# A four-layer graph network kernel: a list sorted by source on the chip, fp32 sums by node, one attention pass

## What is computed

```python
# L0: hyperbolic linear map per node, then a plain sum over the edges
xt = logmap0(proj(mobius_add(proj(mobius_matvec(w, h)), bias)))
x += expmap0(relu(logmap0(proj(expmap0(segment_sum(xt[src], dst))))))
# L1: attention with 4 heads, then 25 steps of a spiking neuron
e = leaky_relu(a_src[src] + a_dst[dst], 0.2); p = exp(e - max_of_destination(e))
x += lif(segment_sum(xw[src] * p, dst) / segment_sum(p, dst) + b) + h
# L2: four edge types; both directions; edges with src == dst left out
x += sum over t of  segment_sum(h[src] * m_t, dst) @ WA[t]  and  segment_sum(h[dst] * m_t, src) @ WB[t], plus x terms
# L3: two graph convolutions with edge weights w (and a loop of weight 1), layer norm behind each
deg = segment_sum(w, dst) + 1; out = dinv * (segment_sum(w * (dinv*h)[src], dst) + dinv*h) + b
```

## Time and profile before

| | |
|---|---|
| median of 3 runs | 9762.14 us (9749.57 to 9762.45) |
| the profiled execution: span from first to last instruction | 9752.6 us |
| busy: PE / weight loads / DVE / ACT / POOL | 3033.5 / 2507.1 / 4339.8 / 1537.8 / 5945.4 us |
| DRAM read / written | 554.98 / 177.15 MB |
| mean granted clock of TensorE, as a share of full speed | 0.559 |

### The profile page before, as it was taken

The page is one execution under the profiler, slowest core; times in us unless marked ns, Lnnn a source line. Parts: engine busy times, 40 slices in busy tenths (PEclk is TensorE's granted clock), DMA queues, the critical chain, the costliest instruction groups (busy, mean ns, idle before and its releaser), DMA issues.

```text
span 9752.6 us, 141440 instructions
## 1 busy us (share of the span) xinstructions
PE 3033.5 (31%) x30372; PEld 2507.1 (26%) x30373; DVE 4339.8 (44%) x10248; ACT 1537.8 (16%) x3193; POOL 5945.4 (61%) x5419
## 2 busy tenths in 40 slices
PE   1122224555311443332232222323242222222221
PEld 1111114555301331012222222222242222222221
DVE  5311135666535997975222222222244333443334
ACT  1000012222101555710111111111120000100000
POOL 0677735777302990007888888888826777367773
PEclk7555557777655555565555555555575555555555
DMA  5322214455322330012333333333343222132221
GB/s 140 84 79 79 79 36 112 133 135 134 96 57 62 99 98 4 1 68 58 61 61 61 61 61 61 61 61 61 61 122 83 78 79 78 38 82 78 78 78 52
DMA packets 578212, 733.23 MB, mean 75 GB/s; under 512 B 158774, under 2 KB 437770, under 8 KB 578138
## 3 DMA queue, kind: packets, MB, share of 16 engines
q0 software_dynamic: 306176, 438.23, 21.0%
q1 hardware_dynamic: 242010, 267.02, 9.4%
q10 hardware_dynamic: 29952, 27.28, 1.1%
HBM read 554.98 MB, written 177.15 MB: 75 GB/s over the span
## 4 chain that ended last, share of the span: by engine, by line
issue 28%; DVE 19%; POOL 15%; PE 15%; DVEq 11%; DMA 8%; ACT 2%; SPq 0%; ACTq 0%; POOLq 0%
POOL GATHERED L599 11%; PE PS L755 8%; DVEq L318 6%; POOL agg_src L665 5%; DMA GATHERED<-typed_tab,IDX 4%; DVE OH L1350 3%; DVE H L1549 2%; DMA agg_src<-MSG,SIDX 2%; PE PS L884 2%; DVE SCR L1344 2%; DVE T L1148 1%; PE PS L809 1%; DVE SM L1158 1%; DVEq L321 1%; DMA GATHERED<-gat_tab,IDX 1%
## 5 line engine op out<-in xcount | busy, mean ns | idle before, releaser
L599 POOL DMA_INDIRECT GATHERED<-row_tab,IDX x2496 | 2372.0, 950 | 1430.6 <-issue 1139.5
L755 PE MATMUL PS<-OH,GATHERED 128*128 128x64 bf16 (+1 forms) x15760 | 1161.1, 253 | 2509.6 <-DVE OH L1350 1561.5
L755 PEld LDWEIGHTS PS<-OH,GATHERED 128*128 128x128 bf16 x15760 | 1022.5, 132 | 2605.9 <-DVE OH L1350 1625.5
L665 POOL DMA_INDIRECT agg_src<-MSG,SIDX x832 | 1331.9, 1601 | 266.8 <-issue 211.4
L599 POOL DMA_INDIRECT GATHERED<-typed_tab,IDX x832 | 879.0, 1056 | 992.0 <-ACT IDX L965 738.9
L599 POOL DMA_INDIRECT GATHERED<-gat_tab,IDX x832 | 785.1, 944 | 452.2 <-issue 229.9
L876 PE MATMUL PS<-EQ,OH 128*128 128x128 bf16 x1024 | 145.7, 294 | 1946.6 <-issue 1707.1
L809 PE MATMUL PS<-IDENT,GATHERED 128*128 128x128 f32 x3328 | 598.7, 356 | 465.9 <-DMA GATHERED<-gat_tab,IDX 349.5
L1807 DVE TENSOR_TENSOR ACC<-ACC,PS 128x128 f32 x256 | 73.7, 288 | 1354.4 <-PE PS L755 1354.4
L809 PEld LDWEIGHTS PS<-IDENT,GATHERED 128*128 128x128 f32 x3328 | 540.4, 187 | 523.9 <-issue 523.8
L969 ACT ACTIVATE IDX<-SRCF 128x4 int32 x816 | 166.9, 205 | 2980.8 <-DMA GATHERED<-row_tab,IDX 2980.8
(11 more groups left out here) (279 smaller groups left out, 6615.0 us busy)
## 6 DMA issues: line engine op xcount, KB each, us to landing
gat_rows<-GATHERED SPq DMA_DIRECT2D x208, 264.0 KB, 2.1
GATHERED<-gat_rows SPq DMA_DIRECT2D x208, 264.0 KB, 2.6
GATHERED<-row_tab,IDX POOLq DMA_INDIRECT x2496
ROWI<-dst_rows ACTq DMA_DIRECT2D x208, 128.0 KB, 3.1
ROWI<-dst_rows SPq DMA_DIRECT2D x208, 128.0 KB, 2.9
ROWI<-key_rows SPq DMA_DIRECT2D x208, 128.0 KB, 3.1
agg_src<-MSG SPq DMA_DIRECT2D x2, 12564.0 KB, 77.3
H<-agg_src SPq DMA_DIRECT2D x98, 256.0 KB, 3.9
```

The source lines that it names most:

```text
L599: pool.indirect_dma_start(out=rows, out_offset=None, in_=table, in_offset=bass.IndirectOffsetOnAxis(ap=IDX[:, k:k + 1], axis=0),).then_inc ...
L665: pool.indirect_dma_start(out=agg_src[k], out_offset=bass.IndirectOffsetOnAxis(ap=SIDX[:, u * CT + t:u * CT + t + 1], axis=0), in_=MSG[:, ...
L755: last = mm(bank(0)[:, 0:o.shape[1]], row_part(t, i), o, start=(n == 0 and t == 0), stop=(n == len(groups) - 1 and t == CT - 1))
```

## The change

- **Sums by node, fp32.** One-hots are 128 x 512 fp32 over a whole block of 128 nodes, and are the stationary operand; the gathered fp32 rows (512 bytes) are the moving one. PE's result has a node on a partition and is added to ACC, T or X directly. `split`, the parts, the windows of 64 and `unload` go. In l0 a column with the edge weight rides along for the degree. In l3 ACT multiplies each gathered row by its weight in place (`weighed_rows`).
- **A list sorted by source.** During walk l0 DVE counts the edges per block of sources (first half: a compare and a reduce over 832 columns every second chunk), works out the starts, and ranks them (second half: a compare, a scan and two more operations of 832 columns every second chunk). POOL then scatters (key, source) pairs, 8 bytes a row, to their places with 832 indirect DMAs, in batches of 16: 96 between l0 and g1 (LISTED_EARLY), 352 behind g1's gathers, 384 when the attention pass is over. Before a batch POOL copies indices and pairs aside and waits for the last batch of the same kind (`listed`).
- **The second typed direction is a walk** ("l2b") over that list: a second typed table is made during walk l2, a block per four chunks (`typed_b`), and gathered by destination and type. `same_keys`, the scatter-add, the copies in DRAM and "back" go. Both walks add straight into X.
- **One attention pass.** "ga", the scores and "gb" become one walk: ACT makes the transposed one-hots (Abs, Relu), PE spreads maxima and scores, DVE does the four small score steps of a chunk (`score`), ACT the Exp, DVE the product (`weigh`), PE and DVE the sums. Where a chunk reaches into a second block, its one-hots and sums are made ahead in buffers of their own (`two`).
- **Typed table.** One fp32 copy per block, even blocks by ACT, odd ones by DVE.
- **Registers.** `read` loads four words; each is passed through a maximum with zero (`kept`) wherever it is used.

```diff
+    typed_b_tab = dram("typed_b_tab", (NB * P * NT4, D))
+    list_dram = dram("list_dram", (NT * P, 2))
...
+                for t in range(BATCH):
+                    pool.indirect_dma_start(out=list_dram,
+                                            out_offset=bass.IndirectOffsetOnAxis(
+                                                ap=PLACE_NOW[:, now + t:now + t + 1], axis=0),
+                                            in_=REC_NOW[:, rec + 2 * t:rec + 2 * t + 2],
+                                            in_offset=None).then_inc(listed[k], 16)
...
+            pool.wait_ge(placed, 1)
+            list_batches(0, LISTED_EARLY)
+            pool.wait_ge(s_stored, 32)
+            walk("g1", gat_tab, XW)
+            list_batches(LISTED_EARLY, LISTED_BESIDE)
+            pool.wait_ge(walks["gb"].added, NCH + 2)
+            list_batches(LISTED_BESIDE, NT // (2 * BATCH))
+            for k in range(SLOTS):
+                pool.wait_ge(typed_stored[k], 16 * (NG * len(range(k, GB, SLOTS)) + 1))
+            walk("l2", typed_tab, D)
+            pool.wait_ge(nb_stored, 16 * (NB + 1))
+            walk("l2b", typed_b_tab, D)
...
-                    pool.tensor_tensor(VROWS[u].rearrange("p (t h d) -> p t h d", t=CT, h=HEADS),
-                                       G3[:, u * CT:(u + 1) * CT, 0:D].rearrange("p t (h d) -> p t h d", h=HEADS),
-                                       EX[:, bass.ds(c * (CT * HEADS), CT * HEADS)]
-                                       .rearrange("p (t h o) -> p t h o", h=HEADS, o=1)
-                                       .to_broadcast([P, CT, HEADS, DH]), ALU.mult).then_inc(v_made, 1)
...
-                            pool.indirect_dma_start(out=agg_src[k],
-                                                    out_offset=bass.IndirectOffsetOnAxis(
-                                                        ap=SIDX[:, u * CT + t:u * CT + t + 1], axis=0),
-                                                    in_=MSG[:, m * P:(m + 1) * P], in_offset=None,
-                                                    compute_op=ALU.add).then_inc(scattered[k], 16)
...
+                pe.wait_ge(ready, k + 1)
+                for t in range(CT):
+                    r = rows(t)
+                    last = mm(bank(to + p)[:, 0:r.shape[1]], onehots_(p, t), r, start=(t == 0), stop=(t == CT - 1))
...
+                    mm(bank(3), NB_HT, WL2[:, (NT4 + 1) * D:(2 * NT4 + 1) * D], start=True, stop=True).then_inc(nb_mm, 1)
+            aggregate("l2", gathered("l2"), gathered_row, parts=((NB, typed_b, None), (NIT - NB, None, None)))
+            aggregate("l2b", gathered("l2b"), gathered_row, table=RANGES_SRC)
...
+                        for t in range(CT):
+                            rows = G3[:, u * CT + t, 0:D]
+                            last = nc.scalar.activation(rows, rows, ACT.Copy, scale=WF[:, bass.ds(c * CT + t, 1)])
+                        last.then_inc(row_weighed, 1)
...
+                nc.scalar.activation(SCRB[:, CE:2 * CE], ROWI[:, u * CE:(u + 1) * CE], ACT.Abs,
+                                     bias=NODE[:, bass.ds(first, 1)], scale=float(FAR)).then_inc(far_made, 1)
+                hold(act, far_made, c + 1)
+                hold(act, adm_ready, c + 1)
+                nc.scalar.activation(EQB[:, p * CE:(p + 1) * CE], SCRB[:, CE:2 * CE], ACT.Relu,
+                                     bias=ONE[:, :], scale=-1.0).then_inc(ot_ready, 1)
...
+            def weights_of(c, u):
+                hold(act, scored, 5 * c + 6)
+                nc.scalar.activation(VX[:, u * CT:(u + 1) * CT, D:XW],
+                                     SCORE[:, (u % 2) * CT * HEADS:(u % 2 + 1) * CT * HEADS]
+                                     .rearrange("p (t h) -> p t h", h=HEADS), ACT.Exp).then_inc(ex_kept, 1)
...
+            def same_bucket(k):
+                return v.tensor_scalar(SAME, BUCKET, KCOL[:, bass.ds(k, 1)], None, ALU.is_equal)
...
+                    v.tensor_reduce(TOTALS[:, bass.ds(k, 1)], SAME, axis=AX.X, op=ALU.add).then_inc(counted, 1)
...
+                    same_bucket(k).then_inc(ranked, 1)
+                    hold(dve, ranked, 4 * k + 2)
+                    v.tensor_tensor_scan(BEFORE, ONE[:, :].to_broadcast([P, NT]), SAME, OFFSETS[:, bass.ds(k, 1)],
+                                         ALU.mult, ALU.add).then_inc(ranked, 1)
+                    hold(dve, ranked, 4 * k + 3)
+                    v.tensor_tensor(BEFORE, BEFORE, SAME, ALU.mult).then_inc(ranked, 1)
+                    hold(dve, ranked, 4 * k + 4)
+                    v.tensor_tensor(PLACEF, PLACEF, BEFORE, ALU.add).then_inc(ranked, 1)
...
+                at_edges(AT3, 2 + u % 2).then_inc(scored, 1)
+                hold(dve, scored, 5 * c + 2)
...
+                hold(dve, wk.gathered[u], rows)
+                v.tensor_tensor(Z3, G3[:, u * CT:(u + 1) * CT, D:XW], AT3[:, :, 0:HEADS], ALU.add).then_inc(scored, 1)
+                hold(dve, scored, 5 * c + 3)
+                v.scalar_tensor_tensor(out=Z3, in0=Z3, scalar=0.2, in1=Z3, op0=ALU.mult, op1=ALU.max).then_inc(scored, 1)
+                hold(dve, scored, 5 * c + 4)
+                v.tensor_tensor(Z3, Z3, AT3[:, :, HEADS:2 * HEADS], ALU.subtract).then_inc(scored, 1)
+                hold(dve, scored, 5 * c + 5)
+                v.tensor_scalar(Z3, Z3, 0.0, None, ALU.min).then_inc(scored, 1)
+            def weigh(c, u):
+                hold(dve, ex_kept, c + 1)
+                v.tensor_tensor(VX[:, u * CT:(u + 1) * CT, 0:D].rearrange("p t (h d) -> p t h d", h=HEADS),
+                                G3[:, u * CT:(u + 1) * CT, 0:D].rearrange("p t (h d) -> p t h d", h=HEADS),
+                                VX[:, u * CT:(u + 1) * CT, D:XW].rearrange("p t (h o) -> p t h o", o=1)
+                                .to_broadcast([P, CT, HEADS, DH]), ALU.mult).then_inc(v_made, 1)
...
+                            if two:
+                                with others((u + 1) % sets):
+                                    b = within(block_values((u + 1) % sets)[2] + 1, NB)
+                                    onehots(c + 1, b, 1 - p, column, second).then_inc(second_onehot, 1)
...
-                    v.tensor_copy(stg[:, 0], src_).then_inc(split2, 1)
-                    hold(dve, split2, n + 1)
-                    v.tensor_tensor(r_, src_, stg[:, 0], ALU.subtract).then_inc(split2, 1)
-                    hold(dve, split2, n + 2)
-                    v.tensor_copy(stg[:, 1], r_).then_inc(split2, 1)
-                    hold(dve, split2, n + 3)
-                    v.tensor_tensor(stg[:, 2], r_, stg[:, 1], ALU.subtract).then_inc(split2, 1)
...
+                    v.tensor_copy(typed_stage(k), bank(2 + t % 6)).then_inc(typed_made[1], 1)
...
+            aggregate("l2", lambda b: X[:, bass.ds(b * D, D)], D, column=DST2[:, :])
+            dve.sem_inc(walks["l2b"].free, RING)
+            dve.wait_ge(list_in, 16)
+            aggregate("l2b", lambda b: X[:, bass.ds(b * D, D)], D, column=LIST_SRC, table=RANGES_SRC)
...
-                split(T[:, 0:NB * D], H[:, 0:NB * D], PARTS, s_tab)
+                dve.sem_inc(s_tab, 1)
                 dve.sem_inc(walks[name].free, RING)
                 dve.wait_ge(s_stored, stored)
-                step(v.memset(ACCT, 0.0))
-                aggregate(name, NP3)
-                step(v.tensor_copy(H3, T3))
-                unload(name)
-                tt(H3, H3, T3, ALU.add)
-                tt(H3, H3, spread(DINV[:, :]), ALU.mult)
+                aggregate(name, lambda b: T[:, bass.ds(b * D, D)], D)
+                tt(H3, T3, spread(DINV[:, :]), ALU.mult)
...
```

## The result

The changed kernel takes **8815.1 us** (median of 4 runs, 8803.8 to 8818.3); the kernel before took 9758.7 in the same comparison, a ratio of 0.9032 (95% interval 0.9019 to 0.9044). The forecast was 8850, so the sum held; its terms did not hold equally well, and two of them, walk l0 and the attention pass, lie outside the ranges that the forecast gave them. The profiled execution spans 8814.8 us, 937.8 less than the one before.

The account below looks back on a forecast made before the run. POOL's indirect DMAs were taken to set the time in walks, DVE's work the time between them. Terms summed to -908 against a span of 9752.6: span 8845, median 8850 us; 8-in-10 range 8620 to 9160.

Parts of the forecast that it names:

- walk l0: Walk l0: gathers stay 832, DVE's ranking fits beside them, small allowances for slips and list steps; +35 (0 to +80).
- the attention pass: Merged attention walk: DVE's chain takes 4.9 us a chunk, 2.9 per further block; 1183 us, +26 (-120 to +215).
- The main term: Stage l2: two walks of 832 gathers replace gathers with scatter-adds, 2102 us instead of 2840.8; -739.
- C: Sorted list: a plain scatter costs as much as the scatter-add, +50 ahead of g1, +249 ahead of l2; 9150; chance 0.16.
- D: Sorted list: 8-byte rows slow the DMA engines, POOL waits at `listed`; some 9900 at 3.6 us a scatter; chance 0.05.
- just hidden: Second half of l0: DVE's work including ranking takes 9.6 of the ring's 10 us per two chunks.
- over 1.0 us on average: Sign that the forecast is wrong: gathers in a walk average over 1.0 us, held by DVE.
- l2 and l3: Walks l2 and l3, paced by POOL's gathers at 1.25 us: l2 -739, both l3 together -94.
- pitch unchanged: Walk l0: gathers with rows of 512 instead of 768 bytes keep POOL's pitch of 1.25 us.
- rival A: Attention pass is short: holds overlap with long operations, DVE at 3.7 us a chunk, 250 less; 8600; chance 0.13.
- B: Attention pass is long: 5.8 us or more a chunk, by register work or ACT table reloads; 9040; chance 0.16.
- To l2: From attention pass to l2: the last scatters, not the typed table, end last; 600 us instead of 683.6, -84.

Follow-up runs that it names:

- P: Changed kernel with the attention pass's last small step standing twice, the second waiting for the first: 10829 us on a slowed chip, 4.72 instead of 4.48 us a chunk.
- the last list experiment: Changed kernel with LISTED_BESIDE 4 instead of 14, 32 scatters beside the attention pass and 704 behind it: 9248 us, 0.9486 of the kernel before.

## Why the prediction was right, and where its steps failed

The main term is right in kind and nearly in size (l2, -739 against -683). That the total came within 35 us is luck: a pass forecast 236 us too long hid gathers and scatters forecast 211 us too short.

- **Tables, the exit of l0, early list, g1**: within 5 us each. Taking the plain scatter as the gather (0.96 + 0.30 us) was the right choice between the two bounds, so rivals C and D fall; at `listed` POOL never waited.
- **Walk l0, +35 against +106.** The step that failed is "just hidden": ranking was weighed as DVE's time against the ring's 10 us, and DVE's time was right (scan 1.95 for 1.9 forecast). What it costs is what it does to the gathers beside it: 416 gathers by 0.22 us, 92 us, and 12 more in the first half (0.974 for 0.945). Over the whole walk the gathers average 1.069 us, so the sign "over 1.0 us on average" was met here, and +106 is outside the term's range of 0 to +80. The row that said so, a 6.49 us gather beside a 6.69 us TENSOR_TENSOR, was used for the scatters around LIF and forgotten for the walks.
- **l2 and l3, 96 us short.** Same step: "pitch unchanged". The 128x512 fp32 one-hots (0.69 us) are longer than the 128x256 bf16 ones; gathers take 0.975 and 0.993 us in l2 and l2b, 832 x (0.030 + 0.048) = 65 us; 0.983 in l3a for 0.950 before, 27 us; 0.976 in l3b for 0.955, 17 us. That is 109 us for the 96 missing, so the other steps of these terms came out some 13 better. The "would be wrong" list had gathers over 1.0 and did not catch these.
- **The pass, 1183 against 947.** The mechanism was right, DVE's chain of small steps, and P shows it; the size was off. A chunk came near my own lower end of 4.2 us (4.27), a second block far below its 2.9, and the term, -210, lies outside its range of -120 to +215. The issue gap with the register work averages 0.85, not 1.15, and stands once; behind the reduce stand 0.38 us, behind the other small steps 0.10 to 0.14 where 0.16 was taken, and nothing ahead of the three long operations (idle times of the groups by line, 2640 to 3560 us, over 206 to 208 chunks). From one chunk's last small step (L1642) to the next one's it is 4.27 us on average where no second block comes in between (159 of them) and 5.05 where one does (48). So a chunk costs 0.63 less than the 4.9 forecast, 131 us, and a second block 0.8, not 2.9, because its one-hots and sums run ahead with no wait: some 100 us more. In time this is nearly rival A, which took 250 us off the pass, and in part by its mechanism, as no gap stands ahead of the long operations; but a chunk did not reach its 3.7, and the total missed its 8600 by what the other terms lost. B fell.
- **To l2, -84 against -40.** Right in kind (the list ends last), wrong by 44 us: scatters beside LIF cost 1.73 us each (254 in 440 us) where 1.58 was taken, and those beside the norm's 6.69 us operations were held as well. The typed table was ready 557 us behind the pass, 576 forecast. So the list ends 86 us behind it, outside the 10 to 40 forecast.

The rule of the Trainium skill, "SBUF — State Buffer", "Who interferes with whom", weighed in the prediction says that `tensor_tensor` doesn't stall descriptor generation, and `tensor_scalar` in its two-port mode does, as whoever has the shared ports keeps them for the whole instruction. The trace agrees for `tensor_scalar` (1.081 us gathers beside compares) and for `tensor_reduce`, which the section says never contends (0.95 at 504.65). It disagrees for `tensor_tensor` with two SBUF inputs (1.37 at 1008.57, 7.33 at 3573.65); the scan, of which the rule says nothing, holds a gather as well (2.44 at 1004.58).

The undisturbed kernel has 86 us left between typed table and list: an estimate is that 62 to 66 scatters more beside the pass would take them away (86 us at the 1.39 of the last list experiment, or at the 1.31 of scatters that nothing holds). It is not measured; the runs that moved scatters there ran slowed.

## What to carry to other kernels

Where POOL's indirect DMAs set the pace, price every DVE operation beside them by what it holds, which grows about with its length squared, and not only by DVE's load. Short operations in place of a long one took the hold away (0.946 us in l2b), and a reduce held nothing; but POOL then waited for DVE on the slowed chips, so no gain in time is on record for it. A chain of small dependent steps is worth counting by its start-to-start distance (0.28 us here), with the long operations behind it at their bare length. And compare a variant only with a reference from the same chip at the same time: the same two kernels differed by 9.7% in one condition and by 2.5% in another.

## What the runs showed that was not expected

In three of the four sets of runs the kernel before took 12 to 14% longer (10973 to 11066 us against 9748 to 9762), on one chip in one set and not in the next. In that condition PE, DVE and SP issue late while POOL issues indirect DMAs, with no wait to be seen, while POOL's own gathers, single instructions and the part of the pass without indirect DMAs keep their times: 2.6 us ahead of a small step of the pass instead of steps 0.28 apart, 193 us instead of 64 for the typed stores, 1534 us from first to last gather in g1 instead of 1040, 1319 and 1272 in l2 and l2b instead of 1064 and 1078. DVE in walk l3b in that condition, one-hots done at 9814.71 and the add 10 us behind them:

```profile
9813.00 0.29 DVE L1279 TENSOR_TENSOR T<-T,PS 128x128 f32 x1 [4.55 <-PE PS L686]
9814.02 0.69 DVE L1261 TENSOR_TENSOR OH<-IOTA,DSTF 128x512 f32 x1 [0.73 <-issue]
9825.02 0.29 DVE L1279 TENSOR_TENSOR T<-T,PS 128x128 f32 x1 [10.30 <-remote]
```

Unrolling didn't cure it. Late delivery of instructions would look like this, but no run shows it, and what puts a chip into the condition stays open. In it the change is worth 2.5% instead of 9.7%: the changed kernel loses 1988 us (10803 less 8815), the kernel before 1307 (11066 less 9759). Of the 1988, 494 are g1's, a walk that both kernels have, and 392 the pass's, where scatters now stand beside chains of short steps. That the pass makes up much of the difference of 681 is likely, but not shown: there is no slowed trace of the kernel before to compare.
